# One graph network of four layers on one core: the square root of the normalisation behind the index copy of a turn's fourth group instead of ahead of it

## What is computed

```
x = layernorm(x + wx * segment_sum(w^2 * wx[src], dst))                          # wx = x @ W.T + b; edges with src != dst
x = layernorm(x + ([x, segment_sum([x[src], attr] @ W1 + b1, dst)] @ W2 + b2))
h = relu(agg(x) @ W1l.T + x @ W1r.T)                                             # agg: weighted sum of sources over deg^2
x = layernorm(x + agg(h) @ W2l.T + h @ W2r.T)
x = layernorm(x + gate(3 steps of a GRU over typed messages, x))
```

## Time and profile before

| what | us |
|---|---|
| median of three runs (13729.97 to 13739.07) | 13733.29 |
| profiled execution: span from the first to the last instruction | 15388.9 |
| pass 1, first gather to last | 4376 to 6134 |
| pass 2 | 6193 to 7868 |
| pass 3 | 7914 to 9730 |
| passes 4 to 6 | 9913 to 15168 |

### The profile page before, as it was taken

One profiled execution on the slowest core, in us unless ns is written; L12 is line 12 of the kernel. 1 busy time (PEld: TensorE's weight loads), 2 busy tenths in 40 slices (PEclk: granted clock), 3 DMA queues, 4 the chain that ended last, 5 costly groups with the idle time before them and its releaser, 6 DMA issues. The chain is left out here.

```text
span 15388.9 us, 172841 instructions
## 1 busy us (share of the span) xinstructions
PE 9965.8 (65%) x37130; PEld 6375.4 (41%) x37131; DVE 6792.6 (44%) x20397; ACT 1404.0 (9%) x4108; POOL 9707.6 (63%) x8863
## 2 busy tenths in 40 slices
PE   6777774444466666555545555588876888677775
PEld 4444444334335444334333333344443444334443
DVE  3333333333367775666656666333332333222223
ACT  1111111111100000000000000100000000000001
POOL 3888887777746666566655555366665666566662
PEclk7555556667787787667767677799997999889887
DMA  8888887777687775677747666477775777467773
GB/s 276 198 198 195 198 180 146 163 162 128 101 223 196 192 193 137 173 192 194 191 125 185 180 180 177 147 210 215 212 195 140 214 212 209 136 183 193 192 191 90
DMA packets 4070001, 2778.79 MB, mean 181 GB/s; under 512 B 430093, under 2 KB 3820298, under 8 KB 4069630
## 3 DMA queue, kind: packets, MB, share of 16 engines
q1 hardware_dynamic: 3529604, 2147.73, 50.7%
q0 software_dynamic: 508368, 612.97, 21.0%
q10 hardware_dynamic: 31722, 15.04, 0.3%
HBM read 2025.54 MB, written 778.19 MB: 182 GB/s over the span
## 5 line engine op out<-in xcount | busy, mean ns | idle before, releaser
L1012 POOL DMA_INDIRECT ring<-t_types,stage x3408 | 3273.1, 960 | 2164.6 <-issue 1349.2
L1012 POOL DMA_INDIRECT ring<-t_x,stage x2272 | 2213.4, 974 | 1450.6 <-issue 887.6
L1544 PE MATMUL bank<-work 128*128 128x512 f32 x5216 | 2624.0, 647 | 596.7 <-DMA work<-t_types 241.1
L1566 PE MATMUL bank<-ring 128*128 128x128 f32 x13632 | 2260.0, 320 | 974.6 <-DMA ring<-t_types,stage 236.2
L1566 PEld LDWEIGHTS bank<-ring 128*128 128x128 f32 x13632 | 2102.0, 229 | 1754.9 <-issue 1461.1
L2032 DVE TENSOR_REDUCE work<-work 128x512 f32<-128x2048 f32 x524 | 1911.5, 3648 | 1012.6 <-DMA work<-t_pairs 931.0
L968 POOL DMA_INDIRECT t_sums<-ring,stage x1136 | 1766.0, 1555 | 432.1 <-issue 262.4
L2007 DVE TENSOR_TENSOR acc<-acc,bank 128x128 f32 x1704 | 480.9, 282 | 3267.0 <-remote 2074.2
L1544 PEld LDWEIGHTS bank<-work 128*128 128x128 f32 x5216 | 1035.5, 210 | 1734.9 <-issue 1378.9
L1012 POOL DMA_INDIRECT ring<-t_h,stage x1136 | 1080.1, 951 | 782.3 <-ACT stage L1214 407.5
L1549 PE MATMUL bank<-work 128*128 128x512 f32 x1048 | 733.6, 788 | 454.8 <-issue 273.3
(11 more groups left out here) (298 smaller groups left out, 11271.9 us busy)
## 6 DMA issues: line engine op xcount, KB each, us to landing
work<-t_pairs SPq DMA_DIRECT2D x2352, 512.0 KB
t_pairs<-acc SPq DMA_DIRECT2D x272, 740.0 KB
t_pairs<-acc SPq DMA_DIRECT2D x272, 370.0 KB
t_pairs<-acc SPq DMA_DIRECT2D x74, 1360.0 KB
work<-t_types SPq DMA_DIRECT2D x294, 256.0 KB
t_types<-work SPq DMA_DIRECT2D x144, 512.0 KB
ring<-t_types,stage POOLq DMA_INDIRECT x3408
ring<-t_x,stage POOLq DMA_INDIRECT x2272
```

The costliest lines, as they stand in the source:

```text
L1012: pool.indirect_dma_start(msg[:, u, :], None, table, bass.IndirectOffsetOnAxis(ap=stage[:, u:u + 1], axis=0)).then_inc(slot_dma[u], 16)
L1544: mm = pe.matmul(bank[4 + half][:, :], dense_t[:, tile, k_ * D:(k_ + 1) * D] if ph > 3 else dense_x[:, tile, :], dense_b[:, half, k_ * 4:( ...
L1566: mm = pe.matmul(bank[q][:, 0:P], msg[:, u, :], hot[:, u, :], start=k_ == 0, stop=k_ == K - 1)
```

## The change

In passes 1 and 3 the part of ScalarE that takes the square root goes behind the copy of the fourth group of the turn (q = 3) and no longer behind that of the third (q = 2). ScalarE's order in the second turn of a pair is now: copy 0, the copies of the step, copy 1, copy 2, copy 3, root. Nothing else is changed.

```diff
             groups(act, lambda at: root(p_l0, at))
-            stage_pass(1, meta_src, 0, {0: rows_turned(True), 2: step_root()})
+            stage_pass(1, meta_src, 0, {0: rows_turned(True), 3: step_root()})
             stage_pass(2, meta_src, 1, {0: rows_turned()})
-            stage_pass(3, meta_src, 2, {0: rows_turned(), 2: step_root()})
+            stage_pass(3, meta_src, 2, {0: rows_turned(), 3: step_root()})
```

## The result

The changed kernel takes 13696.9 us (median of 10 runs, 13690.7 to 13707.5) and the kernel before 13730.1 us (10 runs, 13727.3 to 13740.0). The ratio is 0.9975 [0.9967, 0.9984]: 33 us less, a third of the 102 us forecast.

A forecast was written before the change was run, and what follows sets the result against it. POOL, fed by ScalarE's index copies, was taken as nearest to setting the pace. Pass 3 saves 114 us, other terms zero: 15388.9 to 15275 us profiled, scaled to 102 us off, 13632 us; range 13560 to 13750.

The forecast's parts named there:

- What bounds a pass: Gather passes: POOL, fed by ScalarE's index copies, is nearest to setting the pace; it waits 407.5 us in pass 3.
- forecast floor 1420: POOL in one pass: 1136 gathers issued back to back at 1.25 us each take 1420 us.
- Fourth copy held behind the root, in pass 3 only: ScalarE's root waits 14.8 us for variances in pass 3, holding the fourth copy; POOL stops 7.24 us. Pass 1: none seen.
- The 12 us: Pass 3: the fourth group's copy goes some 12 us before the root, at about 8821.3 and not 8833.71.
- 87, 141, taken 114 us: Pass 3's saving: 87 us from TensorE's 2.64 us wait, 141 us from pass 2's shorter time, middle 114 us.
- forecast 48: Pass 3: the pair of turns falls from 51.5 to about 48 us.
- The root's wait in the new place, pass 1, collisions at zero: VectorE's normalisation wait, pass 1's gain and DMA or engine collisions each taken as 0; bounds 33, 36.9 and 33 us.
- The rival of slower VectorE work or held gathers: Pass 3: moved gathers slow VectorE's scaling-to-variances work, or are held themselves; 13833 us at eight gaps a pair, chance 0.08.
- Gathers of 3.1 us: Moved gathers beside VectorE's work: about 3.1 us instead of 0.62 us by the skill page, a loss of about 3 us a pair.
- the lock-out: POOL's gathers: descriptors cannot be written while VectorE is in a two-port mode; whichever starts first keeps the port pair.
- Scaled alike, 114 x 13733.3 / 15388.9 = 102 us: Whole kernel: the profile's 114 us saving shrinks with the shorter runs' total to 102 us, giving 13632 us.
- The rival of no change: POOL arrives early and waits at the odd turn's first group, or the runs' stall is small; 13706 to 13760, chance 0.34.

The follow-up runs named there:

- the longer chain: Kernel before plus eight value-preserving VectorE instructions ahead of pass 3's combination of the parts, root behind third copy: 13776.9 us (short level), 15458.4 us (long level).
- the early variances: Kernel before with VectorE's part ending in the variances one group earlier in pass 3, root behind third copy: 13692.9 us (short level), 15269.1 us (long level).
- the control: Kernel before with only the two loop bounds loaded with their limits checked, root behind the third copy in both passes: 13730.7 us, ratio 1.0001.
- the two executions named at the start: Two single executions far from both levels, left out of all medians and comparisons: kernel before 19665.6 us, changed kernel 14384.5 us.
- the root one copy ahead: Kernel before with pass 3's root behind the second copy instead of the third: 13815.7 us (short level), 15488.5 us (long level), ratio 1.0065 at both.

## Why the prediction was right or wrong

- **What bounds a pass**: right. POOL fed by the index copies sets the pace at both levels; where nothing holds it, a pass is 1423 us (forecast floor 1420).
- **Fourth copy held behind the root, in pass 3 only**: right. The runs with one half each put the whole gain in pass 3, and the longer chain and the early variances show that it is the variances, through the root, that POOL waits for.
- **The 12 us**: in the steps shown the fourth copy goes 10.4 us ahead of the root at the short level, which is enough, and 6.9 at the long one, the level of the forecast, which is not: POOL still waits 3.37 us for it. The forecast took all that the copy needs to be there at about 8821.3 and saw no other hold at this place.
- **87, 141, taken 114 us**: right in size at its level. The change measured 105 us in a long set. The mean pair fell from 1816 / 35.5 = 51.2 us to 1713.5 / 35.5 = 48.3 us (1136 gathers are 35.5 pairs of 32), forecast 48. That the middle of the two bounds came so near is luck in part: it was a choice, and the gap that stays is split over two places and not one.
- **The root's wait in the new place, pass 1, collisions at zero**: right. The normalisation is not held, pass 1 keeps its time (1494.4 and 1494.2 us), and the gathers take 952 ns as before. The rival of slower VectorE work or held gathers did not show. Gathers of 3.1 us, the figure that the prediction took from the Trainium skill, "SBUF — State Buffer", behind the section "SBUF: two separate sides", are in no trace of pass 3: the longest there is 1.43 us after the change, and 1.46 in the control. This is no test of the lock-out itself. The Trainium skill, "SBUF — State Buffer", section "Who interferes with whom", says that on this chip reductions never take the ports that VectorE shares with GpSimd, and VectorE's long instructions here, of 3.65 us, are reductions.
- **"Scaled alike, 114 x 13733.3 / 15388.9 = 102 us"**: this step failed. It treats the shorter runs as the same execution with every part 11% shorter. They are the same work with POOL's idle taken out: gathers and VectorE's work take the same time, and the gap at the root, beyond its 0.30 us, is 1.2 us a pair and not 7.0. So the runs had 33 x 1.2 = 40 us to give, and gave 33 to 40.
- **The rival of no change** missed by 9 us (its time began at 13706 and the change took 13696.9), but held the right reason: the runs are 1656 us shorter, nearly POOL's 1823 us of idle, "so the stall may be small in the runs". Given that, the sum should have started from the idle that the runs could still hold, 1823 - 1656 = 167 us in six passes together. Pass 1's longer gathers take 1134.7 - 1080.1 = 55 us of it, and 112 us are left for every wait of all six passes: a ceiling, of which 102 us for one wait would have been nearly all.

Left open: why ScalarE's index copies wait longer at the long level, 1381 us in pass 3 against 1033 at the short one. The largest of these waits are, with their us, count and longest, in the changed kernel at the short level and then in the run at the long one:

```profile
ACT stage L1214 <- PE bank L1566: 1023.6, 215, 24.9
```

```profile
ACT stage L1217 <- remote: 732.8, 53, 18.4
```

The changed kernel has no "remote" wait there. No run here changed what a "remote" wait hangs on, so its cause was not tried. TensorE is late too: in pass 2 it idles 245.9 us ahead of its dense products (line 1549) in the profile before, 169.6 us of it with nothing shown that it waits for, and 20.1 us in the changed kernel's. Longer DMA packets do not explain it: on the queue that moves most of the bytes they take 50.7% of 15388.9 us in the one and 57.2% of 13692.2 us in the other, 7802 and 7832 us.

## What to carry to other kernels

A wait on an engine that works in order costs only what it exceeds the lead of whoever is fed from behind it. Measure that lead step by step and add up what is missing (28 us in one pass, nothing in another), not the wait (411 us, of which 40 counted). Before a stall of a profile is turned into a forecast, set the profile's span beside the runs. If they differ by more than the runs' spread, a stall need not scale with the total; here nearly all of the difference was POOL's idle. Bound the stall by the idle that the shorter runs can still hold.

## What the hardware showed that was not expected

The same program has two levels: 13730 us, and 15394 or 15416 us, 12% apart, each with a spread of a few tens of us but for the two executions named at the start. The level stays through a set of runs, for the kernel before and every changed one, and it is no fixed trait of a chip: by the record one chip (number 13) was at the long level in the set of 15394.3 us and, some 38 minutes later, at the short one in the set of 13728.4 us. What sets it is open. The whole difference is in the six gather passes, as idle time of POOL between gathers that in pass 3 take 950 to 952 ns at both. TensorE's mean granted clock is 0.79 at the short level and 0.76 at the long one; in pass 2 it is busy 58 us longer (939.67 against 881.57), of the 252 us by which the pass is longer. The mean clock alone does not make the level: one execution of the change (`third_order33`) had 0.763 and took 13707.9 us. And an edit's worth depends on the level: the change is worth 0.25% at one and 0.67% at the other, the early variances 0.26% and 0.80%, while the longer chain (0.37 and 0.38%) and the root one copy ahead (0.65 and 0.65%) cost the same share at both.
